# Graph layer with routed experts on one core: normalized rows kept as three bf16 pieces, with step, bias and own-row products in bf16

## What is computed

```python
edge_index = stack([src, dst])                       # 100000 edges, sorted by dst; 6250 nodes x 256
# graph part, h = layernorm(x)
msg = segment_sum(h[src], dst);  deg = segment_sum(1, dst)
x1  = x + concat([h, msg / max(deg, 1)], 1) @ W.T + b
# expert part, 8 experts, the best 2 of each row, xn = layernorm(layernorm(x1)) * gamma + beta
logits = xn @ Wr + br;  w = softmax(top2(logits))
y   = sum_e w_e * ( gelu(xn @ W1[e] + b1[e]) @ W2[e] + b2[e] )
out = x1 + y
```

## Time and profile before

| | us |
|---|---|
| median of 3 runs | 1824.79 |
| lowest, highest | 1809.95, 1828.0 |
| profiled execution, own time | 1821.96 |
| its span, first to last instruction | 1820.4 |
| first gather of the stream | 58.9 |
| last gather issued | 1654.0 |

### The profile page before, as it was taken

How to read it: one execution, slowest core, us unless ns; L and a number is a source line. 1 busy time by engine, 2 the same in 40 slices (tenths; PEclk the granted TensorE clock), 3 DMA queues, 4 the chain that set the end, 5 groups by cost and what they waited for, 6 DMA issues and landing times.

```text
span 1820.4 us, 22138 instructions
## 1 busy us (share of the span) xinstructions
PE 1256.1 (69%) x5524; PEld 934.7 (51%) x5524; DVE 775.0 (43%) x2604; ACT 493.1 (27%) x1094; POOL 1125.1 (62%) x1078
## 2 busy tenths in 40 slices
PE   2457774677567765875887577668677576767886
PEld 1234342464346644654666355546465465556775
DVE  9434343343434443444445243543434344446321
ACT  4100031121012320241234123213223232334564
POOL 4556556566656566666666665666666665564567
PEclk9987886786679876897889698878789887888898
DMA  8945343343334334444443343433343343333444
GB/s 262 305 137 160 121 153 99 92 103 104 94 100 112 92 107 103 108 101 106 101 114 95 100 117 90 111 97 98 104 107 100 98 109 94 90 100 80 96 68 47
DMA packets 132619, 203.63 MB, mean 112 GB/s; under 512 B 23948, under 2 KB 100164, under 8 KB 132368
## 3 DMA queue, kind: packets, MB, share of 16 engines
q0 software_dynamic: 64512, 136.52, 30.3%
q1 hardware_dynamic: 64452, 64.36, 11.4%
q10 hardware_dynamic: 3532, 1.34, 0.3%
HBM read 153.66 MB, written 49.27 MB: 111 GB/s over the span
## 4 chain that ended last, share of the span: by engine, by line
PE 40%; issue 19%; another core or an unknown queue 17%; DVE 8%; ACT 7%; DMA 3%; POOL 2%; SPq 1%; DVEq 1%; ACTq 0%; POOLq 0%
PE psum L652 14%; PE psum L745 9%; PE psum L720 7%; PE psum L665 4%; DVE acc L966 3%; POOL out_dram L600 2%; ACT expert_buf L543 2%; PE psum L666 1%; PE psum L699 1%; ACT expert_buf L535 1%; DMA h_rows<-region 1%; PE psum L732 1%; DMA out_dram<-expert_buf,tok_idx 1%; ACT region L479 1%
## 5 line engine op out<-in xcount | busy, mean ns | idle before, releaser
L572 POOL DMA_INDIRECT work<-h_rows,srcs x830 | 794.6, 957 | 478.3 <-issue 194.3
L652 PE MATMUL psum<-work 128*128 128x257 f32 x1660 | 576.1, 463 | 279.5 <-issue 144.6
L966 DVE TENSOR_TENSOR acc<-acc,psum 128x257 f32 x830 | 350.4, 422 | 841.7 <-PE psum L652 404.2
L652 PEld LDWEIGHTS psum<-work 128*128 128x128 f32 x1660 | 324.2, 224 | 423.8 <-issue 389.2
L745 PE MATMUL psum<-region,expert_buf 128*128 x840 | 247.9, 448 | 41.9 <-issue 34.9
L543 ACT ACTIVATE expert_buf<-psum,b_col 128x128 f32<-128x128 f32 x420 | 120.5, 370 | 429.9 <-remote 223.7
L745 PEld LDWEIGHTS psum<-region,expert_buf 128*128 128x128 f32 x840 | 184.8, 229 | 89.3 <-issue 59.4
L720 PE MATMUL psum<-expert_buf 128*128 128x128 f32 x1680 | 214.8, 282 | 3.9 <-issue 2.8
L720 PEld LDWEIGHTS psum<-expert_buf 128*128 128x128 f32 x1680 | 210.7, 199 | 13.2 <-issue 6.6
L592 POOL DMA_INDIRECT out_dram<-expert_buf,tok_idx x76 | 123.5, 1625 | 65.7 <-ACT expert_buf L547 53.1
L665 PE MATMUL psum<-wgt,pair_t 128*128 128x256 f32 x392 | 126.4, 479 | 54.2 <-ACT pair_t L494 43.3
(11 more groups left out here) (196 smaller groups left out, 859.4 us busy)
## 6 DMA issues: line engine op xcount, KB each, us to landing
expert_buf<-queue SPq DMA_DIRECT2D x105, 130.0 KB
work<-h_rows,srcs POOLq DMA_INDIRECT x830
region<-in_L_ffn_W_dram SPq DMA_DIRECT2D x16, 512.0 KB
h_rows<-region SPq DMA_DIRECT2D x7, 896.0 KB
x_rows<-region SPq DMA_DIRECT2D x7, 896.0 KB
own<-h_rows SPq DMA_DIRECT2D x49, 128.0 KB
own<-x_rows SPq DMA_DIRECT2D x49, 128.0 KB
out_dram<-acc SPq DMA_DIRECT2D x49, 128.0 KB, 2.6
```

The costliest lines, as they stand in the source:

```text
L572: pool.indirect_dma_start(grow[:, t % RING, 0:D], None, h_rows, bass.IndirectOffsetOnAxis(srcs[:, t:t + 1], 0)).then_inc(got[t % RING], 16)
L652: summed.up(pe.matmul(STEP_BANKS[t % BANKS][:, 0:GW], hot[:, k, :], grow[:, t % RING, :], start=True, stop=True))
L966: added.up(dve.tensor_tensor(sums, sums, STEP_BANKS[t % BANKS][:, 0:GW], ALU.add))
```

## The change

The normalized row is kept as three bf16 numbers whose sum is the f32 value. `h_rows` and the ring `grow` have 768 bf16 columns in place of 256 f32 ones (1536 bytes a row, before 1024), and `hot` is bf16.

- **Step:** three bf16 matmuls (257, 256 and 256 columns) into one bank in place of one f32 matmul of 257.
- **Own rows:** six bf16 products with the identity in place of two f32 transposes.
- **Biases:** `gnn_b` and `b2` are split into three bf16 rows (`three_rows`) and added by one bf16 product with three rows of ones. For `b2` the product opens the sum of the expert's second product, so VectorE scales the result straight from PSUM by the row's weight; ScalarE's L547 and VectorE's reading of expert numbers into registers are gone, and `SENT_AT` is one step earlier.
- **Head:** ScalarE normalizes in place and copies the first piece, GpSimd subtracts it, VectorE makes the second and third (`more_pieces`). Staging has seven places, partly in memory of `acc` and `work`; ScalarE clears `acc` in three parts. The first destinations are loaded as 112 x 7, compared with 50 bounds and counted by 14 small matmuls. `x_rows` is copied from `x` in DRAM.

```diff
+    PIECES = 3
+    DP = PIECES * D
...
-    h_rows = nc.dram_tensor("h_rows", (NT * P, D), F32).ap()
+    h_rows = nc.dram_tensor("h_rows", (NT * P, DP), BF16).ap()
...
-        SENT_AT.append(t + 4 + AHEAD if t + 4 + AHEAD < STEPS else max(t + 5, STEPS + 4, SENT_AT[-1] + 2))
+        SENT_AT.append(t + 3 + AHEAD if t + 3 + AHEAD < STEPS else max(t + 4, STEPS + 4, SENT_AT[-1] + 2))
...
@@ sync_head
-            sp.dma_start(x_rows[b * LB * P:(b + 1) * LB * P, :].rearrange("(t p) d -> p t d", p=P), xall[:, b * LB:(b + 1) * LB, :]).then_inc(s_xrows, 16)
+            sp.dma_start(x_rows[rows, :], x[rows, :]).then_inc(s_xrows, 16)
...
@@ scalar_head
+        acc_zero.up(act.copy(acc[:, 0:EARLY, :], zcol[:, 0:1].unsqueeze(1).broadcast_to([P, EARLY, GW])))
         for b in range(NLB):
...
-            for j in range(LB):
-                t = b * LB + j
-                i = act.activation(hst[b % 2][:, j, :], xall[:, t, :], ACT.Identity, bias=nmr[:, t:t + 1], scale=rstd[:, t:t + 1])
-            h_up.up(i)
+            for t in range(b * LB, (b + 1) * LB):
+                i = act.activation(xall[:, t, :], xall[:, t, :], ACT.Identity, bias=nmr[:, t:t + 1], scale=rstd[:, t:t + 1])
+            a_own.then(i)
...
+            first_up.up(act.copy(hst[b][:, :, 0:D], xall[:, b * LB:(b + 1) * LB, :]))
...
+        for parts, lo, hi in (((0, 1, 2), EARLY, LATE), ((5,), LATE, NT)):
+            for b in parts:
+                act.wait_ge(s_hst[b], 16)
+            i = act.copy(acc[:, lo:hi, :], zcol[:, 0:1].unsqueeze(1).broadcast_to([P, hi - lo, GW]))
+        acc_zero.up(i)
...
@@ scalar_stream
-            for j in results(t - 2):
-                yb_up.wait(act, j)
-                ys_up.up(act.activation(ysb[j % YB], ysb[j % YB], ACT.Identity, scale=wcol[:, j % YB:j % YB + 1]))
...
@@ gpsimd_head
-        acc_zero.up(pool.memset(acc[:, :, :], 0.0))
+        for b in range(NLB):
+            if b == 2:
+                source_tables()
+            first_up.wait(pool, b)
+            group = xall[:, b * LB:(b + 1) * LB, :]
+            rest_up.up(pool.tensor_tensor(group, group, hst[b][:, :, 0:D], ALU.subtract))
...
@@ gpsimd_stream
-                pool.indirect_dma_start(grow[:, t % RING, 0:D], None, h_rows,
+                pool.indirect_dma_start(grow[:, t % RING, 0:DP], None, h_rows,
...
@@ tensor_head
-        pe.matmul(psum[0][0:NT, 0:512], ones[0:1, 0:NT], fst_f[0:1, 0:512], start=True, stop=True)
-        spread.up(pe.matmul(psum[1][0:NT, 0:FIRSTS - 512], ones[0:1, 0:NT], fst_f[0:1, 512:FIRSTS], start=True, stop=True))
+        for side in range(2):
+            for g in range(FG):
+                i = pe.matmul(psum[0][0:NT, side:side + 1], under[0:FS, g, side:side + NT], ones[0:FS, 0:1], start=(g == 0), stop=(g == FG - 1))
+        spread.up(i)
...
@@ tensor_stream
-                summed.up(pe.matmul(STEP_BANKS[t % BANKS][:, 0:GW], hot[:, k, :], grow[:, t % RING, :], start=True, stop=True))
+                sums, rows = STEP_BANKS[t % BANKS], grow[:, t % RING, :]
+                pe.matmul(sums[:, 0:GW], hot[:, k, :], rows[:, 2 * D:DP + 1], start=True, stop=False)
+                pe.matmul(sums[:, 0:D], hot[:, k, :], rows[:, D:2 * D], start=False, stop=False)
+                summed.up(pe.matmul(sums[:, 0:D], hot[:, k, :], rows[:, 0:D], start=False, stop=True))
...
-                    pe.transpose(PAIR[:, c * P:(c + 1) * P], own[:, 0, c * P:(c + 1) * P], ident[:, :])
+                    for piece in range(PIECES):
+                        pe.matmul(PAIR[:, c * P:(c + 1) * P], own_h[:, piece * D + c * P:piece * D + (c + 1) * P], ident_b[:, :],
+                                  start=(piece == 0), stop=(piece == PIECES - 1))
...
+                pe.matmul(PAIR[:, 0:D], ones_b[0:PIECES, :], gb_rows[:, :], start=True, stop=False)
                 for c in range(2 * DC):
-                    pe.matmul(PAIR[:, 0:D], pair_t[:, c * P:(c + 1) * P], wgt[:, c, :], start=(c == 0), stop=False)
-                prod_up.up(pe.matmul(PAIR[:, 0:D], ones[0:1, :], gb_row[0:1, :], start=False, stop=True))
...
+                pe.matmul(result(j), ones_b[0:PIECES, :], b2_rows[:, ds(e, 1), :].rearrange("p a o -> p (a o)"), start=True, stop=False)
                 gel_up.wait(pe, j)
...
+    def more_pieces(b):
+        group = xall[:, b * LB:(b + 1) * LB, :]
+        rest_up.wait(dve, b)
+        d_own.then(dve.tensor_copy(hst[b][:, :, D:2 * D], group))
+        h_up.up(dve.tensor_tensor(hst[b][:, :, 2 * D:DP], group, hst[b][:, :, D:2 * D], ALU.subtract))
+
+    def three_rows(rows, full):
+        d_own.then(dve.tensor_copy(rows, full))
+        for n in range(2):
+            d_own.then(dve.scalar_tensor_tensor(full, rows, less_piece[0:PIECES, n:n + 1], full, ALU.mult, ALU.add))
+            i = dve.tensor_copy(rows, full)
+            if n == 0:
+                d_own.then(i)
+        return i
...
@@ vector_stream
+            if 118 <= t < 118 + X:
+                if t == 118:
+                    dve.wait_ge(s_b2, 16)
+                b2_up.up(three_rows(b2_rows[:, t - 118, :], b2_t[:, t - 118, :]))
...
-                if j in UPTO:
-                    expert[batch_of(j)] = experts(dve, "v", batch_of(j))
-                e = expert[batch_of(j)][j - UPTO[batch_of(j)]]
                 y_up.wait(dve, j)
                 row_up.wait(dve, j)
-                yb_up.up(dve.tensor_tensor(ysb[j % YB], result(j), b2_bc[:, ds(e, 1), :].rearrange("p a o -> p (a o)"), ALU.add))
+                ys_up.up(dve.tensor_scalar(ysb[j % YB], result(j), wcol[:, j % YB:j % YB + 1], None, ALU.mult))
```

204 lines of the change are left out of this document (123 added, 81 removed).

## The result

After the change the kernel takes 1850.2 us (median of 4 runs, 1845.5 to 1856.6), before it 1824.3 us (4 runs on the same chip). The ratio is 1.016, with a 95% interval of 1.010 to 1.022. Measured twice more, further down, the ratio was 1.023 (1.016 to 1.029) and 1.021 (1.016 to 1.027). So the change makes the kernel slower, by about 2%. I had forecast 1786 us, a gain. The time lies inside the range that I gave, but on the wrong side of the kernel before.

The account below looks back on a forecast made before the run. The loop of step matmul L652 and add L966 was taken to pace the stream, GpSimd's gathers hardly on the path. Terms -56 - 17 + 6 + 4 - 12 + 10 + 15 + 18 - 4 = -36 gave 1786 us, range 1710 to 1885.

Parts of the forecast that it names:

- late signals: Stream: VectorE's add waits 288.6 us for events with no named sender, TensorE's record finished but signal unseen; left unchanged.
- Step matmuls, -56: Stream: three bf16 passes take 0.78 of two f32 ones; 22% of L652's 253 us on the chain, -56 us.
- Head, +18: Before the first gather: -13 + 25 + 2 + 4 us, moving it from 59 to about 77; +18 us (0, +35).
- Registers -12: VectorE no longer reads expert numbers into registers: -12 us (-15, 0).
- L547 0: L547 leaves ScalarE, which has slack; GpSimd waited 53.1 us for it but is not the bound: 0 (-20, 0).
- tail -4: End of the kernel: one hop less between result and GpSimd's write, one slot earlier: -4 us (-12, 0).
- Biases -17: L666's two f32 passes become one bf16 pass; it has 24 us of the chain: -17 us (-24, -8).
- Clock, +15: TensorE, busy less, gets the high clock less often; a fall by 0.035 costs +15 us (0, +40).
- Transfers 0: Stream: 54 MB more is gathered, DMA share stays near 0.5: 0 us (0, +25).
- B: Rival: late signals shrink with f32, half of them may go, 143 us more, 1643 us; chance 0.08.
- D: Rival: slower, as late signals grow with the number of TensorE instructions, +108 us, 1894 us; chance 0.30.
- C: Rival: gain eaten, VectorE paces every burst, half of the 56 us arrives, head at +26, 1822 us; chance 0.20.

Follow-up runs that it names:

- the counting part: The kernel before with tile edges counted by small matmuls, the clear of the sums on ScalarE and scales within the next group's statistics: ratio 0.997.
- the other order: The kernel after with subtraction on VectorE, middle-piece cast on ScalarE, square roots one group ahead, small loads by SyncE and other head edits: 1831.0 us, ratio 1.0075.
- its variant: The kernel after with one step matmul in place of three and adds of 129 columns, on the quick chip: ratio 1.028.
- narrow gathers: The kernel after with gathers of 1024 bytes a row in place of 1536, the third piece a constant in SBUF: ratio 1.010.

## Why the prediction was wrong, point by point

- **What bounds the kernel.** "GpSimd's gathers are hardly on the path" came from its 2% of the chain and its 271 us of waits for a slot. Without the late signals the picture is another: on the quick chip the stream is GpSimd's list to within 1%. On the slower ones taking 147 us off that list gains some 80 us. I had the floor in hand and read it only as a limit to gains.
- **Step matmuls, -56.** This step failed. The ratio of durations was right (0.77 measured), the share on the path was wrong: I took the 253 us of the chain as a price. On the slower chips the whole stream gained under 30 us (-27.3 in the profiled pair), and in two of three comparisons of medians about 10; going from three passes to one moved the time not at all. Halving the same instruction in before on the quick chip moved it 2 us. My explanation, argued and not shown: where a ring of slots stands between engines, the chain passes through whichever engine is busy at the moment.
- **Head, +18.** The second failed step, and the one that decided the sign. It measured +48.7. The terms: the -13 for the counting part was -2.9 when it was made alone in before (the last store of the rows held the first gather there, with or without tables). VectorE's fourteen operations took 2.0 us each, 28 us for my 25, and ScalarE's copies 1.69 us: right. GpSimd's subtraction took 3.4 to 4.3 us where I had 1.5 to 2.9 from the clear. "4 for what the engines wait for one another" was the main error: some 19 us of waits behind GpSimd and a round of five engine changes for each of seven groups. That the two together make the rest is read from the timeline; what each is worth was not measured by itself, beyond the 4.8 us of the subtraction on VectorE and the 18.8 us of the other order. The upper end, +35, stood beside a rule that the trace now bears out in part. SBUF — State Buffer of the Trainium skill (Who interferes with whom) says that a VectorE copy, cast or tensor_scalar that runs in a two-port mode, and one with two inputs in SBUF against a GpSimd instruction that reads SBUF, contends with GpSimd. Here tensor_scalar and two-input operations of seven columns waited out whole subtractions (3.08 us, and 7.50 across two), but the cast to bf16 at 91.63 did not wait (2.01 us), and it was the casts that I had priced. Even the upper end was 14 us short of the 48.7.
- **Registers -12, L547 0, tail -4.** Alone, on the quick chip, -2 us with an interval of -5 to +1. There GpSimd's waits for L547 and the registers were worth nothing; on a slower chip they were not tried. The tail of after is 2 us longer on the slower chip; on the quick one that of its variant is 4 us shorter.
- **Biases -17, own rows +6, `b2` +4, `three_rows` +10.** Not separated; with the step, the registers and the clock they make the stream's -27 of the profiled pair.
- **Clock, +15.** Right as far as it was measured. In the profiled pair it fell by 0.049; over the runs of the two later measurements by 0.034 and 0.037, where I had 0.035. What it took back could not be measured by itself. Two readings of the earlier trace rows were loose. That the clock was low there is an inference from the 1.20 us of a step, since steps take 1.06 to 1.20 us at the granted clock 0.50 later on: the trace has no granted clock before 113 us, and the views print 1.00 there. And before's step was there to be read at the high level: 0.60 us by its two records, 0.43 us from one to the next.
- **Transfers 0.** Right (narrow gathers: no gain). **Late signals unchanged.** Right within 20 us (289 to 308), so B and D both fell.
- **The rivals.** The outcome has C's signature, the gain eaten and a longer head, but not its mechanism: half the add gains nothing, so VectorE does not pace the bursts. Its price, 1822 us, had the head at +26. No rival had the head as the thing that turns the sign; with its upper end of +35 the sum was 1803, and of the 43 us still missing to the profiled 1845.5 us 14 are the head's, 23 the stream's and 6 the tail's.

## What to carry to other kernels

A share of the chain is not a price when rings of buffers join the engines: first write down each engine's full list with its gaps, and if one list is within a few per cent of the stage, price every other edit at nothing until shown otherwise. Work added ahead of a stage that is bound in this way costs its whole latency (the head's 18.8 us came through as 19.2), and that latency is the round over the engines, group by group, not the sum on the fullest of them. When a large wait has no named sender, ask how the kernel looks without it, since it may hide the true bound. And compare two streams by more than one profile of each: the same kernel gave 1551, 1562 and 1568 us.

## Not expected of the hardware

- The same program took 1522 us on one chip and 1798 to 1824 us on others, with single operations of the same length on both (gather 949 ns, add 422 ns). In the traces the difference is idle time: 286 us of long gaps on GpSimd in the stream in one, 4 us in the other.
- A GpSimd subtraction of 1792 columns held up VectorE's smallest operations for its whole length (0.17 us became 3.08, and 7.50 with two subtractions in a row), while a cast from f32 to bf16 of 1792 columns beside it kept its 2.01 us. It took 3.4 to 3.6 us, and 4.3 us in the two cases where it began while a two-input operation of VectorE was running.
- Three bf16 passes of 256 columns with their weight loads follow one another in 0.33 us at the granted clock 1.00, 0.11 us apart, though each record says 0.27 us; there the sum of the records, 0.81 us, is more than twice the time.
- The mean granted clock followed the work given to TensorE: 0.759, 0.783 and 0.862 with one, three and five passes a step.
